# Startup loads in another order, and VectorE makes part of the gate logits of a graph-and-experts layer

## The chip, the cores and the metric

The kernel runs on one core of one Trainium2 chip. Its time is the device time of one execution in microseconds (us); smaller is better. TensorE (PE) does the matmuls, its weight loads are listed as PEld, VectorE is DVE, ScalarE is ACT, GpSimd is POOL. SyncE (SP) computes nothing here: it issues most of the DMAs, one after the other in its queue; ACT and POOL issue the rest.

## The reference

There are 3125 tokens (rows) of 256 numbers and a sparse graph of 53125 weighted edges among them. The layer is

```
xn = layernorm(x)
# graph part, adj[dst, src] += weight
h  = adj @ xn
a0 = softmax((adj @ h) @ W0.T + b0)            # 128 wide
a1 = softmax((adj @ [a0, a0]) @ W1.T + b1)
x  = x + tanh([a0, a1] + h) + linear_attention(xn)
# experts part
xn2 = layernorm(x)
logits = xn2 @ gate_w + gate_b                 # 8 experts, top 1, capacity 489
buf[e, slot] = xn2 of the tokens of expert e
y   = relu(buf @ w1[e] + b1[e]) @ w2[e] + b2[e]   # 256 -> 1024 -> 256
x   = x + y[token] * prob[token]
```

## The kernel before

Everything is in f32 and written out by hand: each engine has one queue of instructions whose order is fixed in the code, and semaphores carry the waits. Tokens are cut into 25 tiles of 128.

**Start.** SP loads all of `dst`; from it DVE works out where in the sorted edge list each tile begins (`base_i`). With these numbers SP loads a window of edges per tile, three small DMAs each (`window`, L436), in four groups of tiles, `GROUPS = ((0, 2), (2, 6), (6, 16), (16, 25))`. Group 0 is written out, the others are loops on SP. Behind group 0 SP issues the loads of `x` (L454, L457) and of five weights (`wo`, `wq`, `W0`, `W1`, `b1`; L461); behind group 1 eleven gate weights, biases and other constants (L451); then groups 2 and 3. All sixteen weights and constants count on one semaphore, `s_w`. ACT loads the first 7 tiles of `x` and two weights at the very start, and then loads its activation table (L670). ACT turns the integers of a group of windows into floats in `cast` (L700 to L702), at the end of the turn before the one in which DVE's `prepare` uses them.

**Build.** A software pipeline over `it`: per turn DVE makes one-hot tiles, PE multiplies them to dense 128x128 blocks of the adjacency matrix (`build`, L1464), ACT copies them out (`evac`) and they are stored to DRAM and at once applied to xn (`apply`, L1481). During the first 25 turns edges are sorted into slots as well (`spread`, `slot`, `ranks`, `slots`), and keys and values are made (`turn`, `product`, `squares`, `kvprod`). PE turns the five weights in `others()`, at `it == 1`, after a wait for all of `s_w`.

**Two layers.** The dense matrix streams back through a ring of five 1280 KB slots (L542), and PE multiplies it per strip of four tiles (`strip(l, k, inserts)`, L1631: 25 steps `j` per strip, two records each). Between the steps of strip `k` of layer 1 PE executes inserts for earlier strips: `turns` (L1647), `gate_turn(k - 1)` at step 23 (8 transposes of finished rows X1, L1385), `logits(k - 2)` at step 2 (16 records, L1667), `counts(k - 2)` at step 10 (L1676 to L1684). ACT copies the transposed rows out (`xtout`, L817). DVE's order for each strip is `chosen(k - 2)` (bias and choice of expert, starts with L1263), `biased(k - 1)` (L1217), `summed`, `finished` (L1233), `moments`, `root`, `slotted(k - 2)`, `prob(k - 2)`, `normal(k - 1)` (L1286, writes the normed rows XN). The last three strips have two, two and one tile and an order of their own. POOL scatters each normed row to its slot of an expert's buffer in DRAM (L636) and its residual row (L643).

**Experts.** After some matmuls whose results are not used (`WARM`, L1733), for each of the 8 experts PE does `up` (L1719, 8 blocks `f` of 128 hidden units), ACT the relu of each block (L864), PE `down` (L1730, four token blocks `c`, 8 steps `f` each), DVE the output rows (`yblock`), POOL the scatter to `out`. SP loads an expert's tokens with `tokens` in four quarters (L515) and their residual rows with `kept_rows` (L518); DVE transposes the tokens in `columns` (L1370).

Of the kernel before, what the change touches and what calls it, by code (L numbers as in the profile page):

```python
# [17 lines left out]
H = 128  # L18
P = 128
NT = 25  # L20
NE = 8
# [26 lines left out]
NWL = 16  # L48
# [14 lines left out]
NGT = len(GATES)  # L63
WARM = 11
# [44 lines left out]
def graph_program(nc, a, out):  # L109
    ctx = ExitStack()  # L110
    with ctx:
# [110 lines left out]

        iota_n = sb("iota_n", [P, P])
# [116 lines left out]
        s_w = sem("s_w")  # L340
        s_wt = sem("s_wt")
# [31 lines left out]
        s_xn2 = sem("s_xn2")  # L373
        s_nb = sem("s_nb")
# [51 lines left out]
        def _(sp):  # L426
# [10 lines left out]
            for g, (t0, t1) in enumerate(GROUPS):  # L437
                if g == 0:
                    for j in range(t0, t1):
                        window(g, j)  # L440
                else:
                    with sp.Fori(t0, t1) as j:
                        window(g, j)
                if g == 1:
                    for to, src in ((gate_w[:, :, :], half("L0_ffn_gate_w")), (bo_b[:, :], a["L0_mix_bo"].partition_broadcast(P)), (gb1_b[:, :], a["L0_gnn_b1"].partition_broadcast(P)),
# [12 lines left out]
                if g == 0:  # L458
                    for to, src in ((wo_n, half("L0_mix_wo")), (wq_n, half("L0_mix_wq")), (W0_n, a["L0_gnn_W0"]),
                                    (W1_n, a["L0_gnn_W1"]), (b1_n, a["L0_ffn_b1"])):  # L460
                        sp.dma_start(to, src).then_inc(s_w, 16)  # L461
# [50 lines left out]
            def tokens(e, s):  # L512
                blocks = xbuf_dram[ds(e * XS, XS), :].rearrange("(b j) (q f) -> q j b f", j=32, q=4)
                for q in range(4):
                    sp.dma_start(xbs[32 * q:32 * q + 32, s, :, :], blocks[q]).then_inc(s_tok[s], 16)  # L515
# [10 lines left out]
            for l in (0, 1):  # L526
                for q in range(NC):
# [14 lines left out]
                    sp.dma_start(RING[:, slot_of[g % 5], 0:w], adj_dram[q, :, 0:w]).then_inc(s_ald[g % 5], 16)  # L542
                    if g == 10:
# [7 lines left out]
            tokens(0, 0)  # L551
            tokens(1, 1)
            sp.wait_ge(s_dres, 16 * NT)
            kept_rows(0, 0)
            before(0, NT)
# [108 lines left out]
        def _(act):  # L664
            half = lambda name: a[name].rearrange("(r p) n -> p r n", p=P)
            act.dma_start(X1[:, 0:XG[0][1], :], a["x"][0:XG[0][1] * P, :].rearrange("(j p) d -> p j d", p=P)).then_inc(s_x[0], 16)
            act.dma_start(wk_n, half("L0_mix_wk")).then_inc(s_kvw, 16)
            act.dma_start(wv_n, half("L0_mix_wv")).then_inc(s_kvw, 16)
            act.wait_ge(s_const, 2)
            nc.scalar.activation(rsum[:, 0, 0:1], ones_f[:, 0:1], ACT.Sqrt)  # L670
# [88 lines left out]
            for it in range(NU + 3):  # L759
# [24 lines left out]
                if it == 1:  # L784
# [25 lines left out]
            def xtout(k):  # L810
# [3 lines left out]
                n, i0 = len(Z1[k]), Z1[k][0] - GATES[g][0]  # L814
                for b in range(i0 // 2, (i0 + n + 1) // 2):
# [944 lines left out]
```

## Time and profile before

| | |
|---|---|
| time, median of 3 runs | 1199.76 us (1198.54 to 1200.06) |
| the profiled execution's own time | 1197.42 us |
| its span in the profile | 1195.6 us |
| PE busy | 1112.7 us, 93% of the span |
| DVE busy | 708.8 us, 59% |
| ACT busy | 316.0 us, 26% |
| POOL busy | 166.6 us, 14% |
| DMA | 175.37 MB, 147 GB/s over the span |

The profile is of one execution. Busy times are sums over the whole span, which has stages with different limits; "idle before" is time that an engine stood still ahead of an instruction, and the arrow behind it names what released it. Ends of matmuls are modelled. The stages are: start and sorting to about 200 us, build to 629, layer 0 to 775, layer 1 to 947, experts to the end.

### The profile page before, as it was taken

Reading aid. Unit: us, or ns where it says so; the run is one execution under the profiler, and the core shown is the slowest. Engines: PE = TensorE matmul, PEld = TensorE weight load, DVE = VectorE, ACT = ScalarE, POOL = GpSimd, SP = SyncE. Lnnn points to the kernel's source line nnn. Section 1 sums busy time; section 2 is a strip of 40 time slices with the busy share of each in tenths; the row PEclk is TensorE's granted clock in tenths of the full one; section 3 lists DMA queues with packets and bytes.
Section 4 is the critical chain, followed back from the end, with each engine's and each line's share of the span. In section 5 each row is a group of like instructions: output and inputs, shape, how many; then the busy total and the mean of one; then the engine's idle time right before and its main releaser. Section 6 shows DMA issues by size and latency. Waiting matters only on the chain.

```text
span 1195.6 us, 14060 instructions
## 1 busy us (share of the span) xinstructions
PE 1112.7 (93%) x4867; PEld 700.0 (59%) x4867; DVE 708.8 (59%) x1563; ACT 316.0 (26%) x1035; POOL 166.6 (14%) x206
## 2 busy tenths in 40 slices
PE   3589989999999999999998999999999699999995
PEld 2356656666666666666683444545558456666664
DVE  7798999998786877768740010204536334554443
ACT  3468767521212212112220111101112111222220
POOL 1013223301010100000000000000333511111111
PEclk9789989999999999999998999999999799999998
DMA  5111110122323333332238988787884564555510
GB/s 162 18 12 46 45 45 18 72 88 90 140 103 139 122 121 127 120 156 94 88 116 318 350 314 306 267 309 267 300 305 149 159 199 113 117 141 131 136 58 7
DMA packets 78724, 175.37 MB, mean 147 GB/s; under 512 B 33567, under 2 KB 62010, under 8 KB 66622
## 3 DMA queue, kind: packets, MB, share of 16 engines
q1 hardware_dynamic: 68462, 124.02, 32.8%
q10 hardware_dynamic: 6064, 42.40, 8.8%
q0 software_dynamic: 4128, 8.04, 1.9%
q8 instruction: 41, 0.67, 0.2%
q14 instruction: 29, 0.24, 0.1%
HBM read 113.82 MB, written 63.09 MB: 148 GB/s over the span
## 4 chain that ended last, share of the span: by engine, by line
PE 80%; DVE 9%; issue 3%; ACT 3%; another core or an unknown queue 2%; SPq 2%; DMA 1%; POOL 0%; POOLq 0%; DVEq 0%; ACTq 0%
PE ps L1481 20%; PE ps L1631 18%; PE ps L1464 11%; PE ps L1730 9%; PE ps L1719 9%; PE ps L1448 2%; PE ps L1507 2%; PE ps L1385 2%; PE ps L1434 2%; DVE W L983 1%; PE ps L1483 1%; PE ps L1733 1%; DVE RY L979 1%; ACT W L715 1%
## 5 line engine op out<-in xcount | busy, mean ns | idle before, releaser
L1481 PE MATMUL ps<-RING,XX 128*128 128x512 f32 x600 | 283.1, 594 | 0.3 <-ACT RING L743 0.3
L1631 PE MATMUL ps<-RING,RY 128*128 128x512 f32 (+2 forms) x750 | 277.5, 527 | 4.6 <-issue 4.6
L1631 PEld LDWEIGHTS ps<-RING,RY 128*128 128x128 f32 x750 | 134.0, 192 | 131.2 <-issue 129.1
L1464 PEld LDWEIGHTS ps<-RING 128*128 128x128 f32 x1250 | 163.7, 193 | 45.8 <-issue 44.7
L743 ACT COPY RING<-ps 128x512 f32<-128x512 f32 (+1 forms) x157 | 91.6, 584 | 317.0 <-PE ps L1464 300.7
L1464 PE MATMUL ps<-RING 128*128 128x128 f32 x1250 | 171.1, 278 | 0.5 <-ACT RING L733 0.5
L1481 PEld LDWEIGHTS ps<-RING,XX 128*128 128x128 f32 x600 | 102.9, 191 | 73.2 <-issue 72.0
L1023 DVE TENSOR_TENSOR RING<-iota_n,RY 128x512 f32<-128x512 f32 (+1 forms) x157 | 108.0, 688 | 43.6 <-PE ps L1464 38.9
L1029 DVE TENSOR_TENSOR RING<-iota_n,RY 128x512 f32<-128x512 f32 (+1 forms) x157 | 117.3, 747 | 0.0
L864 ACT ACTIVATE RY<-ps,b1T 128x489 f32<-128x489 f32 x64 | 42.8, 669 | 179.7 <-PE ps L1719 178.7
L1032 DVE TENSOR_TENSOR RING<-RING,RY 128x512 f32<-128x512 f32 x132 | 90.2, 683 | 0.0
L1358 DVE SCALAR_TENSOR_TENSOR W<-ps,RING,W 128x256 f32<-128x256 f32 (+1 forms) x32 | 15.5, 484 | 111.1 <-PE ps L1730 110.1
L636 POOL DMA_INDIRECT xbuf_dram<-XX,sidx x25 | 24.7, 989 | 345.1 <-DVE sidx L1298 339.6
L1202 DVE TENSOR_REDUCE nmx<-ps 128x4 f32<-128x512 f32 (+1 forms) x7 | 4.4, 634 | 113.9 <-PE ps L1385 113.9
L622 POOL TENSOR_TENSOR XX<-XX,bo_b 128x256 f32<-128x256 f32 x25 | 29.3, 1173 | 255.0 <-PE ps L1464 255.0
L1730 PE MATMUL ps<-RING,RY 128*128 128x256 f32 (+1 forms) x256 | 56.3, 381 | 3.0 <-ACT RY L864 3.0
L1730 PE MATMUL ps<-XT,RY 128*128 128x256 f32 (+1 forms) x256 | 56.3, 381 | 3.0 <-ACT RY L864 3.0
L659 POOL DMA_INDIRECT out<-W,RING x32 | 31.3, 978 | 198.0 <-DVE W L1365 181.3
L1730 PEld LDWEIGHTS ps<-RING,RY 128*128 128x128 f32 (+1 forms) x256 | 47.1, 185 | 13.8 <-ACT RY L864 6.2
L1730 PEld LDWEIGHTS ps<-XT,RY 128*128 128x128 f32 (+1 forms) x256 | 47.1, 185 | 13.7 <-ACT RY L864 6.2
L1719 PE MATMUL ps<-RING,XT 128*128 128x489 f32 x128 | 53.2, 574 | 1.5 <-issue 1.5
L1448 PE MATMUL ps<-wkvT,XT 128*128 128x512 f32 x100 | 50.9, 633 | 4.0 <-ACT XT L706 4.0
(251 smaller groups left out, 1268.3 us busy)
## 6 DMA issues: line engine op xcount, KB each, us to landing
RING<-adj_dram SPq DMA_DIRECT2D x62, 1280.0 KB
adj_dram<-RING ACTq DMA_DIRECT2D x31, 1280.0 KB, 4.6
rbuf_dram<-W SPq DMA_DIRECT2D x8, 516.0 KB, 5.5
RING<-rbuf_dram SPq DMA_DIRECT2D x8, 516.0 KB, 4.1
xbuf_dram<-W SPq DMA_DIRECT2D x8, 512.0 KB, 3.2
XT<-in_L_ffn_w SPq DMA_DIRECT2D x16, 256.0 KB
XT<-in_L_ffn_w SPq DMA_DIRECT2D x4, 1024.0 KB
RING<-in_L_ffn_w SPq DMA_DIRECT2D x16, 256.0 KB
```

Of the source, the lines that this page charges most:

```text
L659: gp.indirect_dma_start(out[:, :], bass.IndirectOffsetOnAxis(ap=rbs[0:n, e % 2, c, D + 1:RES].bitcast(I32), axis=0), ybs[0:n, e % 2, c, :] ...
L743: nc.scalar.copy(RING[:, n % 2, u % 5 * 512:u % 5 * 512 + w], ps[:, u % 2, 0:w]).then_inc(s_bev, 1)
L864: nc.scalar.activation(hmT[:, f, 0:CAPX], ps[:, 2 + f % 3, 0:CAPX], ACT.Relu, bias=b1T[:, f, e:e + 1]).then_inc(s_hidv, 1)
L1023: v.tensor_tensor(h[:, 0, 0:n, :], every, grid(0), ALU.is_equal).then_inc(s_eq, 1)
L1029: last = v.tensor_tensor(h[:, 1, 0:n, :], every, grid(1), ALU.is_equal)
L1032: last = v.tensor_tensor(h[:, 0, 0:n, :], h[:, 0, 0:n, :], grid(2), ALU.mult)
L1448: last = nc.tensor.matmul(ps[:, PROD, :], XT[:, c, m * P:(m + 1) * P], wkvT[:, c, :], start=(c == 0), stop=(c == 1))
L1464: last = nc.tensor.matmul(o[:, i * P:(i + 1) * P], h[:, 0, i, :], h[:, 1, i, :], start=True, stop=(j != s))
L1481: last = nc.tensor.matmul(ps[:, ACC + dd, :], w, at, start=(j == 0), stop=True, skip_group_check=True)
L1631: last = nc.tensor.matmul(o, (Y if l == 0 else S0)[:, j, :], RING[:, slot_of[g % 5], i * across + first:i * across + first + w], start=(j ...
L1719: last = nc.tensor.matmul(ps[:, 2 + f % 3, 0:CAPX], w1s[s][:, c, f * P:(f + 1) * P], xbT[:, s, c, 0:CAPX], start=(c == 0), stop=(c == 1))
L1730: last = nc.tensor.matmul(o, hmT[:, f, c * P:c * P + n], w2s[s][:, f, :], start=(f == 0), stop=(f == 7))
```

## The change

Six edits are made together.

1. ACT loads its activation table ahead of its three DMAs, not behind them.
2. The four windows of group 1 are written out on SP instead of looped over. The five weights go behind them, ahead of the constants, on a semaphore of their own (`s_wt5`); PE waits for these alone, at `it == 2` instead of 1, and ACT's copies move with it.
3. For the first two tiles of each of the first four strips of layer 1, the gate logits come from DVE: a new `dots(k)` after `normal(k)`, 16 multiply-and-add-up instructions over 256 elements. PE's transposes and logits of these tiles, and one of ACT's two copies per strip, are gone. The gate weights come in spread over all partitions (1024 KB, issued on SP in layer 1 behind load `NC + 5` of the ring), and DVE reorders them once.
4. `counts` moves from step 10 (12 in strip `ka`) to step 15.
5. The tokens of expert 0 are issued half on SP and half on ACT, and the residual rows of expert 0 go ahead of the tokens of expert 1.
6. `down` waits for the relu blocks one at a time in its first token block, instead of for all eight ahead of it.

```diff
-NWL = 16
+NWL = 11
+DOTS, DOT_TILES = 4, 2
+        gwb = HB[:, 0:16, 0:H].rearrange("p t (f e) -> p t f e", e=NE)
+        gwT = RY[:, 3250:5298].rearrange("p (e f) -> p e f", e=NE)
+        junk = xtf[:, 6144:6400]
...
@@ SP, start
-                if g == 0:
+                if g < 2:
                     for j in range(t0, t1):
                         window(g, j)
...
                 if g == 1:
+                    for to, src in ((wo_n, half("L0_mix_wo")), (wq_n, half("L0_mix_wq")), (W0_n, a["L0_gnn_W0"]),
+                                    (W1_n, a["L0_gnn_W1"]), (b1_n, a["L0_ffn_b1"])):
+                        sp.dma_start(to, src).then_inc(s_wt5, 16)
...
-                if g == 0:
-                    for to, src in ((wo_n, half("L0_mix_wo")), (wq_n, half("L0_mix_wq")), (W0_n, a["L0_gnn_W0"]),
-                                    (W1_n, a["L0_gnn_W1"]), (b1_n, a["L0_ffn_b1"])):
-                        sp.dma_start(to, src).then_inc(s_w, 16)
@@ SP, ring loads
+                    if g == NC + 5:
+                        sp.wait_ge(s_sum[0], 4)
+                        sp.dma_start(HB[:, 0:16, 0:H], a["L0_ffn_gate_w"].rearrange("f e -> (f e)").partition_broadcast(P).rearrange("p (t r) -> p t r", t=16)).then_inc(s_gwb, 16)
@@ SP, experts
-            tokens(0, 0)
-            tokens(1, 1)
+            tokens(0, 0, (0, 1))
             sp.wait_ge(s_dres, 16 * NT)
             kept_rows(0, 0)
+            tokens(1, 1)
@@ ACT
+            act.wait_ge(s_const, 2)
+            nc.scalar.activation(rsum[:, 0, 0:1], ones_f[:, 0:1], ACT.Sqrt)
             act.dma_start(X1[:, 0:XG[0][1], :], ...).then_inc(s_x[0], 16)
             act.dma_start(wk_n, half("L0_mix_wk")).then_inc(s_kvw, 16)
             act.dma_start(wv_n, half("L0_mix_wv")).then_inc(s_kvw, 16)
-            act.wait_ge(s_const, 2)
-            nc.scalar.activation(rsum[:, 0, 0:1], ones_f[:, 0:1], ACT.Sqrt)
...
-                if it == 1:
+                if it == 2:
                     others_out()
...
+                if k < DOTS:
+                    n, i0 = n - DOT_TILES, DOT_TILES
...
+            act.wait_ge(s_disp, 16 * NT)
+            for q in (2, 3):
+                act.dma_start(xbs[32 * q:32 * q + 32, 0, :, :], ...[q]).then_inc(s_tok[0], 16)
@@ DVE, layer 1
+                if k < DOTS:
+                    dotted = slice(GATES[k][0], GATES[k][DOT_TILES])
+                    v.tensor_tensor(tb8[:, dotted, :], tb8[:, dotted, :], gate_b[:, :].unsqueeze(1).to_broadcast([P, DOT_TILES, NE]), ALU.add)
+                for i, j in list(enumerate(GATES[k]))[DOT_TILES if k < DOTS else 0:]:
...
+            def dots(k):
+                dve.wait_ge(s_xn2, k + 1)
+                for j in GATES[k][:DOT_TILES]:
+                    for e in range(NE):
+                        link(v.scalar_tensor_tensor(out=junk, in0=XN[:, j, :], scalar=1.0, in1=gwT[:, e, :], op0=ALU.mult, op1=ALU.mult, accum_out=tb8[:, j, e:e + 1]))
+            dve.wait_ge(s_gwb, 16)
+            link(v.tensor_copy(gwT.rearrange("p e (t r) -> p t r e", t=16), gwb))
...
                 normal(k - 1)
+                if k - 1 < DOTS:
+                    dots(k - 1)
@@ PE
             def others():
-                pe.wait_ge(s_w, 16 * NWL)
+                pe.wait_ge(s_wt5, 16 * 5)
...
-                if it == 1:
+                if it == 2:
                     others()
...   gate_turn and logits
-                for j in Z1[k]:
+                for j in Z1[k][DOT_TILES if k < DOTS else 0:]:
...
-                    inserts[10] = [later(counts, k - 2)]
+                    inserts[15] = [later(counts, k - 2)]
...   strip ka: counts from step 12 to 15
             def down(e, s):
-                pe.wait_ge(s_hidv, 8 * e + 8)
                 for c in range(4):
...
                     for f in range(8):
+                        if c == 0:
+                            pe.wait_ge(s_hidv, 8 * e + f + 1)
```

## Rows read from the trace of the kernel before

**Rows 1.** The page, busy time of each engine: us, share of span, instructions.
```profile
PE 1112.7 (93%) x4867; PEld 700.0 (59%) x4867; DVE 708.8 (59%) x1563; ACT 316.0 (26%) x1035; POOL 166.6 (14%) x206
```

**Rows 2.** The chain that ended last: start us, us, what.
```profile
36.15 3.07 DMA cols<-in_L_mix_ln_k_b
...
818.40 0.87 PE ps L1385 x8
...
822.71 1.69 PE ps L1667 x16
```

**Rows 3.** Timeline of the start: start us, us, engine line op, idle before and releaser.
```profile
2.41 1.28 ACT L670 ACT_TABLE_LOAD   x1 [2.41 <-issue]
...
6.16 0.18 DVE L907 CAST W<-W 125x17 f32<-125x17 int32 x1 [1.93 <-DMA W<-in_dst]
...
9.41 0.41 SPq L436 DMA_DIRECT2D HB<-in_src  x1
...
11.52 0.34 SPq L436 DMA_DIRECT2D HB<-in_src  x1
...
15.92 2.33 SPq L461 DMA_DIRECT2D RING<-in_L_mix_wo  x1
...
21.63 0.36 SPq L436 DMA_DIRECT2D HB<-in_src  x1
...
24.23 0.35 SPq L436 DMA_DIRECT2D HB<-in_src  x1
...
32.82 0.20 DVE L946 TENSOR_SCALAR W<-HB 128x72 f32<-128x72 f32 x1 [4.51 <-ACT HB L702]
...
37.70 0.37 SPq L436 DMA_DIRECT2D HB<-in_src  x1
...
51.69 0.27 DVE L893 RECIPROCAL lna<-lnr 128x18 f32<-128x18 f32 x1 [3.39 <-ACT lnr L689]
...
65.38 0.34 SPq L436 DMA_DIRECT2D HB<-in_edge_weight  x1
...
67.27 0.33 ACT L700 CAST HB<-HB 128x180 f32<-128x180 int32 x1
...
69.15 0.40 DVE L995 RECIPROCAL hta<-hrs 128x40 f32<-128x40 f32 x1
```

**Rows 4.** Busy time of each engine in one stretch of layer 1, clock, DMA.
```profile
778.00:803.00 25.00, 25.00 (x66) 11.58 (x65) 0.00 (x0) 0.58 (x1) 0.00 (x0) 1.00 0.86 312
```

**Rows 5.** Instructions of two DVE lines: count, ns least/median/most, span of starts.
```profile
L1128 DVE SCALAR_TENSOR_TENSOR HB<-HB x1: 628/628/628, 328.9 to 328.9; 128x450 bf16<-128x450 f16 x1
L1128 DVE DVE_READ_ACCUMULATOR HB<-HB x1: 84/84/84, 329.4 to 329.4; 128x1 f32 x1
...
L1362 DVE SCALAR_TENSOR_TENSOR W<-W x32: 424/426/427, 978.7 to 1185.0; 128x256 f32<-128x256 f32 x24, 105x256 f32<-105x256 f32 x8
```

**Rows 6.** Timeline of layer 1, as rows 3.
```profile
824.43 0.63 DVE L1263 SCALAR_TENSOR_TENSOR wkvT<-ps,wkvT,gate_b 128x8 f32<-128x8 f32 x4 [9.83 <-PE ps L1667]
...
876.39 0.63 DVE L1263 SCALAR_TENSOR_TENSOR wkvT<-ps,wkvT,gate_b 128x8 f32<-128x8 f32 x4 [10.54 <-remote]
...
899.90 0.63 DVE L1263 SCALAR_TENSOR_TENSOR wkvT<-ps,wkvT,gate_b 128x8 f32<-128x8 f32 x4 [8.35 <-remote]
...
908.41 1.09 PE L1385 MATMUL ps<-ident,XX 128*128 128x128 f32 x8 [0.41 <-DVE XX L1233]
...
938.73 0.79 PE L1647 MATMUL ps<-W1T,W 128*128 128x128 f32 x2 [5.32 <-ACT W L795]
```

**Rows 7.** Timeline from layer 1 to the experts.
```profile
953.55 4.32 SPq L515 DMA_DIRECT2D RING<-xbuf_dram  x8
...
958.84 1.30 DVE L1370 STREAM_TRANSPOSE RING<-RING 128x512 f32<-128x512 f32 x2 [10.28 <-DMA RING<-xbuf_dram]
...
959.70 13.36 PE L1719 MATMUL ps<-RING,XT 128*128 128x489 f32 x32 [1.54 <-issue]
```

**Rows 8.** Groups by line: busy, mean ns, idle before, releaser.
```profile
L1730 PE MATMUL ps<-XT,RY 128*128 128x256 f32 (+1 forms) x256 | 56.3, 381 | 3.0 <-ACT RY L864 3.0
```

More of the change, by code:

```diff
@@ L340, in graph_program @@
         s_w = sem("s_w")
+        s_wt5 = sem("s_wt5")
         s_wt = sem("s_wt")
@@ L373, in graph_program @@
         s_xn2 = sem("s_xn2")
+        s_gwb = sem("s_gwb")
         s_nb = sem("s_nb")
@@ L510, in weights, with tokens @@
                 sp.dma_start(w2s[s], a["L0_ffn_w2"][ds(e, 1), :, :].rearrange("a (c p) f -> p (a c) f", p=P)).then_inc(s_wl[s], 16)
-            def tokens(e, s):
+            def tokens(e, s, quarters=(0, 1, 2, 3)):
                 blocks = xbuf_dram[ds(e * XS, XS), :].rearrange("(b j) (q f) -> q j b f", j=32, q=4)
-                for q in range(4):
+                for q in quarters:
                     sp.dma_start(xbs[32 * q:32 * q + 32, s, :, :], blocks[q]).then_inc(s_tok[s], 16)
@@ L864, in hidden @@
                     nc.scalar.activation(hmT[:, f, 0:CAPX], ps[:, 2 + f % 3, 0:CAPX], ACT.Relu, bias=b1T[:, f, e:e + 1]).then_inc(s_hidv, 1)
+            act.wait_ge(s_disp, 16 * NT)
+            for q in (2, 3):
+                act.dma_start(xbs[32 * q:32 * q + 32, 0, :, :], xbuf_dram[0:XS, :].rearrange("(b j) (q f) -> q j b f", j=32, q=4)[q]).then_inc(s_tok[0], 16)
             for e in range(NE):
@@ L1261, in chosen @@
                 dve.wait_ge(s_lg, k + 1 if k < NGT - 1 else NZ)
-                for i, j in enumerate(GATES[k]):
+                if k < DOTS:
+                    dotted = slice(GATES[k][0], GATES[k][DOT_TILES])
+                    v.tensor_tensor(tb8[:, dotted, :], tb8[:, dotted, :], gate_b[:, :].unsqueeze(1).to_broadcast([P, DOT_TILES, NE]), ALU.add)
+                for i, j in list(enumerate(GATES[k]))[DOT_TILES if k < DOTS else 0:]:
                     last = v.scalar_tensor_tensor(out=tb8[:, j, :], in0=ps[:, LGB, i * NE:(i + 1) * NE], scalar=nr[:, 1, j:j + 1], in1=gate_b[:, :],
@@ L1663, in logits @@
                 ge(pe, s_lgr, g)
-                for j in Z1[k]:
+                for j in Z1[k][DOT_TILES if k < DOTS else 0:]:
                     i = j - GATES[g][0]
@@ L1701, in _ @@
                 strip(1, k, inserts)
-            strip(1, ka, {1: [later(logits, ka - 2)], 3: [later(turns, 1, ka - 1)], 12: [later(counts, ka - 2)], 21: [later(gate_turn, ka - 1)]})
+            strip(1, ka, {1: [later(logits, ka - 2)], 3: [later(turns, 1, ka - 1)], 15: [later(counts, ka - 2)], 21: [later(gate_turn, ka - 1)]})
             strip(1, kb, {3: [later(turns, 1, ka)], 4: [later(logits, ka - 1)], 14: [later(counts, ka - 1)], 22: [later(gate_turn, ka)]})
```

## The prediction

> **What bounds the kernel now.** I read the page first, then the chain that ended last, then the timeline at the places that the edits touch. The page says that PE is busy for 93% of the span [rows 1], so in the build and in the two layers only less work on PE, or an end to one of its waits, pays. The chain says where PE isn't the bound. At the start it goes through SP's queue and ends in the landing of the last constant at 39.2 us, for which PE's `others()` waits [rows 2]. Late in layer 1 it turns into DVE's work on the gate, and in the experts it is PE again, with a short ACT step between `up` and `down`. So four places matter: the start, the gate's share of PE in layer 1, the step to the experts, and that ACT step. I take each by itself, as PE's or DVE's order joins them in one line: what comes earlier at one place stays earlier behind it.
>
> **The start.** PE's 12 us wait for the constants looks like the prize, but it isn't all to be had. Follow what is late next. With the wait gone, the first turns go as fast as DVE and the windows allow, and DVE waited in two places: 4.51 us for the cast of group 1, whose windows now come earlier, and 3.39 us for ACT's root, which was late behind PE at 32.82 and 51.69 [rows 3], 7.9 us together. But ACT's `cast` of group 2 starts at 67.27, when the last DMA of that group, issued at 65.38, has just landed (1.9 us) [rows 3]. Before the change that load had nothing to spare, so from here on the start can only gain what SP's queue gains. DVE's step behind the cast (69.15) shows no idle time ahead of it: DVE and the windows were level.
>
> What SP's queue gains up to the first window of group 2, at 37.70 [rows 3]:
> - The four windows of group 1. In the loop one starts 2.60 us after the other (21.63 to 24.23), written out 2.11 us (9.41 to 11.52) [rows 3]. 4 x 0.49 = 2.0 us.
> - `dst`. DVE waits 1.93 us for it, until 6.16 [rows 3], and all of SP's queue hangs on this. It shares the DMA engines with the three loads that ACT issues at once; now these come behind the 1.28 us table load [rows 3]. Bounds 0 and 1.93 (DVE isn't free sooner); I take 1.5, since `dst` is by far the smallest of them and needs only a little lead.
> - The weight `wo` takes 2.33 us to issue, a window's DMA 0.34 to 0.41 [rows 3]: SP is held up behind the large loads of x. Behind the windows it may cost little; or the first window pays in its place. Bounds 0 and 2.0, I take 0.8, between the two.
> - The order of the five weights and the constants costs nothing more: all were ahead of 37.70 already.
>
> Sum 4.3 us, bounds 2.0 and 5.9; I add 0.2, as DVE then waits for the windows where it was level with them: 4.5 us. The cover of the rest: ACT's x, `wk` and `wv` come some 1 to 2 us later and push DVE's first work back by as much, which the 7.9 us less the 4.5 us hold. `others()` at turn 2 is 15 short PE records while DVE still prepares group 1; its weights are issued right behind the windows of group 1 and land about when that work starts. Group 3's windows come as much earlier on the same queue. The build after it is bound by PE and DVE and keeps the 4.5 us.
>
> **The gate in layer 1, what PE sheds.** Eight transposes take 0.87 us, sixteen logit records 1.69 us [rows 2], 2.56 us per strip; half of it goes in four strips: 4 x 1.28 = 5.1 us. One of ACT's two copies goes too, off the path.
>
> **What DVE pays.** `dots` is 16 linked instructions per strip, each a SCALAR_TENSOR_TENSOR over 256 f32 with an accumulator read. The same instruction without the read takes 426 ns; the one pair in the trace takes 628 ns for 450 elements and its 84 ns read ends with it [rows 5]. Both fit one line of (628 - 426) / 194 = 1.05 ns per element, so the read seems hidden. With the 0.03 us that a linked neighbour starts later: 0.46 us. If the read came in full behind it, 0.54. I take 0.48, nearer to the pair: 16 x 0.48 = 7.7 us per strip. They stand behind `normal`, where DVE idles before `chosen` for 9.8, 10.5 and 8.4 us [rows 6] (three of the four stand there). PE now delivers the logits 1.28 us earlier, so 8.5, 9.2 and 7.1 us are free. The first three groups fit. The fourth doesn't: `chosen(3)`, at 899.90, can move up by 3 x 1.28 = 3.84 us from the strips before, and in its own strip by 8.35 - 7.7 = 0.65 us instead of 1.28. That matters, because from there the path is DVE's: PE waits 0.41 us for DVE's `finished` at 908.41 [rows 6]. So layer 1 gains 3.84 + 0.65 = 4.5 us; 4.9 at 0.46 us per dot, 3.5 at 0.54.
>
> `counts` at step 15 lies later than one-hot rows that come earlier than now, so PE doesn't wait in it, and `slotted`, which needs it, stands behind `root`: nothing. The 1 MB of gate weights (1024 KB) and DVE's reordering (2048 elements, 3.4 us at eight times the 426 ns row) fall where DVE is idle for 25 us and the DMA engines are 0.86 busy at 312 GB/s [rows 4]. At that rate the extra MB takes 3.4 us in a ring whose loads are asked for four chunks of ten records ahead, 15 us at 66 records in 25 us [rows 4]. Hidden; without the ring's lead it would be 3.4 us once. SP waits for `s_sum` there, which layer 0 has long given.
>
> The Trainium skill speaks against this edit: its page "Vector Engine (DVE) Microarchitecture Reference", section "Points that are easy to get wrong", says that this instruction with two SBUF sources that aren't bf16 halves its throughput. L1362 is such an instruction, without an accumulator, and a slope of 1.05 ns from a bf16 pair to it shows no halving; with the accumulator on f32 no run here shows it. By the rule the sum is the second rival's.
>
> **To the experts.** PE waits 1.54 us after its unused matmuls, until DVE's transpose has begun on expert 0's tokens; DVE waits for the last of four quarters, issued 0.54 us apart (8 in 4.32 us) [rows 7]. With two on each queue the last is issued 1.1 us earlier, and expert 1's no longer follow on its heels. Bounds 0 (the landing is what takes the time, not the issue) and 1.54; I take 1.0. Expert 1's tokens now wait for the residual scatter, which is done well before PE has finished expert 0.
>
> **`down`.** PE stands still 3.0 us for the relu in this group and 3.0 in its twin over the other weight buffer [rows 8], 6.0 in all, 0.76 per expert. The relu of block 7 is the last; seven of the eight steps of the first token block now stand in front of it, and it has only 0.76 us left to run. All 6.0 us go. Seven more waits per expert on PE's queue cost at most what the like waits in `up` do, where no idle time is listed. DVE's output rows wait for PE, not the other way round: what hides them stays.
>
> **The sum.** 4.5 + 4.5 + 1.0 + 6.0 = 16.0 us. The profiled execution took 1197.42 us around its span of 1195.6, 2.3 below the median of the runs; the saving is a difference, so I put it on the median: 1199.76 - 16.0 = 1183.8 us.
>
> **Rivals.**
> 1. *SP's queue stays as long.* `dst` lands no earlier and the wait of `wo` only moves to the windows: the start gives 2.0, and with dots at 0.54 us layer 1 gives 3.5: 12.5 us, 1187.3. For it: every byte of x still has to pass. Chance 0.18.
> 2. *The accumulating form runs at half rate.* The streaming part, 256 x 1.05 = 0.27 us, doubles: 0.46 + 0.27 = 0.73 us per dot, 11.7 per strip. Then DVE never idles between groups: from `chosen(2)` at 876.39 to the end of its work at 891.55 is 15.2 us, so a group takes 26.9, and from 814.60 (824.43 - 9.83) `chosen(3)` starts at 814.6 + 11.7 + 3 x 26.9 = 907.0, 7.1 later than before. 4.5 + 1.0 + 6.0 - 7.1 = 4.4 gained: 1195.4. Against it: rows 5. Chance 0.08.
> 3. *The other side: dots that take more than 0.81 us each.* In that formula `chosen(3)` is late by 64 c - 39.8 us; it eats the other 11.5 us from c = 0.80. At twice the whole row, 0.85 + 0.03 = 0.88, it is 16.5 late: 5 us slower, 1204.8. Chance 0.04.
> 4. *A stall that goes.* Near 933 us PE, DVE, ACT and SP all stand still; PE for 5.32 us before 938.73 [rows 6], and ACT, named as releaser, was waiting too. Nothing in the profile explains it. If the new order of PE's work clears it, 4.6 us more: 1179.2. Chance 0.08.
> 5. *The start isn't bound where I think*, and the edits give back what they gain to within a measurement. Chance 0.02.
>
> The forecast has 0.60: its own range is 1181 to 1187. To reach 8 in 10 I take in rivals 1 and 4: 1178.5 to 1191. A measurement of this kernel can tell about 0.2%, 2.4 us. Faster by more: 0.60 + 0.18 + 0.08 + 0.08 = 0.94; within: 0.02; slower: 0.04.
>
> **What would show it.** Right: group 2's cast near 62.8 with ACT idle ahead of it; dots at 0.46 to 0.50 us apart; `chosen(3)` directly behind the last of them, and the first three with idle time before them; PE waiting about 1.3 us for `finished(4)`; no idle time at L1730; a gap under 0.8 us before the first `up`. Wrong: a cast near 65 (rival 1), dots apart by over 0.6 us, PE idle in the ring while the gate weights load, or a clock below full speed in the early turns, if PE now stands still longer before the group 2 windows.

## The result, and the profile after

The changed kernel takes 1177.26 us, median of four runs (1176.02 to 1178.36), beside 1199.15 us for the kernel before on the same chip: a ratio of 0.9818, 95% interval 0.9801 to 0.9835, or 21.9 us less. The prediction was 16.0 us less, 1183.8, with 1178.5 as its low end: the direction was right, the size too small. The profiled execution took 1178.36 us around a span of 1176.6, so the two traces stand 19.0 us of span apart (the traced execution of the kernel before, 1197.42 us, is faster than all of its four runs, that of the changed kernel is the slowest of its four).

The page of the changed kernel, busy time of each engine:

```profile
PE 1109.7 (94%) x4819; PEld 697.4 (59%) x4819; DVE 738.8 (63%) x1688; ACT 315.3 (27%) x1031; POOL 167.6 (14%) x206
```

DVE has 30 us more work than in [rows 1], nearly all of it the new dots (64 of 0.467 us). The start, in the timeline of the changed kernel, answers to [rows 3]:

```profile
0.81 1.28 ACT L676 ACT_TABLE_LOAD   x1 [0.81 <-PEq L1778]
1.25 0.44 ACTq L677 DMA_DIRECT2D XX<-in_x  x1
...
5.04 0.30 DVE L921 CAST W<-W 125x17 f32<-125x17 int32 x1 [0.80 <-DMA W<-in_dst]
...
8.43 0.41 SPq L443 DMA_DIRECT2D HB<-in_src  x1
...
15.67 1.39 SPq L443 DMA_DIRECT2D HB<-in_src  x1
...
20.78 0.35 SPq L443 DMA_DIRECT2D HB<-in_src  x1
...
22.81 0.35 SPq L443 DMA_DIRECT2D HB<-in_src  x1
...
24.16 0.43 SPq L454 DMA_DIRECT2D RING<-in_L_mix_wo  x1
...
34.35 0.37 SPq L443 DMA_DIRECT2D HB<-in_src  x1
...
59.41 0.34 SPq L443 DMA_DIRECT2D HB<-in_edge_weight  x1
...
61.07 0.34 ACT L709 CAST HB<-HB 128x180 f32<-128x180 int32 x1 [3.12 <-DMA HB<-in_edge_weight]
...
62.56 0.40 DVE L1009 RECIPROCAL hta<-hrs 128x40 f32<-128x40 f32 x1 [2.33 <-ACT hrs L781]
```

`dst` lands 1.1 us earlier (DVE had waited for it until 6.16, now until 5.04), although ACT's load of x is issued during the table load and not behind it. The windows of group 1, written out, stand 2.03 us apart. The issue of `wo` fell from 2.33 to 0.43 us, but the first window of group 1 now pays 1.39. Group 2's first window comes 3.35 us earlier, its last DMA 5.97 (65.38 to 59.41), and the cast 6.2 (at 61.07, where the prediction had 62.8), with 3.12 us of idle time on ACT ahead of it.

DVE in layer 1: the last dot of the first group, then `chosen(0)`; the last dot of the fourth group, then `chosen(3)`; and PE at `gate_turn(4)`:

```profile
813.51 0.42 DVE L1327 SCALAR_TENSOR_TENSOR XT<-XX,RY 128x256 f32<-128x256 f32 x1
813.86 0.08 DVE L1327 DVE_READ_ACCUMULATOR XT<-XX,RY 128x1 f32 x1
815.04 0.17 DVE L1278 TENSOR_TENSOR wkvT<-wkvT,gate_b 128x16 f32<-128x16 f32 x1 [1.09 <-PE ps L1694]
...
885.90 0.42 DVE L1327 SCALAR_TENSOR_TENSOR XT<-XX,RY 128x256 f32<-128x256 f32 x1
886.36 0.17 DVE L1278 TENSOR_TENSOR wkvT<-wkvT,gate_b 128x16 f32<-128x16 f32 x1
...
895.43 1.09 PE L1412 MATMUL ps<-ident,XX 128*128 128x128 f32 x8 [0.88 <-DVE XX L1247]
```

The picture is the forecast one: idle time behind the first group's dots, none behind the fourth's, PE 0.88 us late for `finished(4)`. Against [rows 6] `chosen(3)` comes 13.5 us earlier, 8.1 of it the start's (the transpose for which PE waits at the start of layer 1 is at 775.11 and 766.98). That leaves 5.4 us for layer 1 up to there, where the sum had 4.5. But 1.7 of the 5.4 are a delay that is gone, not work saved. In the kernel before, on this chip, DVE began `chosen(3)` (899.90) 1.69 us after PE's logits were done:

```profile
896.36 1.85 PE L1667 MATMUL ps<-gate_w,XT 128*128 128x8 f32 x16
```

The reorder of the gate weights took DVE 2.35 us, at 782.10, and PE has no idle time in the ring there.

Then something that the change isn't about. The timeline of PE and ACT, and below it the stretch behind the stall (us, busy time of PE, PEld, DVE, ACT, POOL, granted clock, DMA share, GB/s):

```profile
910.83 0.60 PE L1412 MATMUL ps<-ident,XX 128*128 128x128 f32 x4
...
915.61 0.59 ACT L828 COPY XT<-ps 128x512 f32<-128x512 f32 x1 [9.72 <-remote]
...
917.46 0.90 PE L1674 MATMUL ps<-W1T,W 128*128 128x128 f32 x4 [4.05 <-issue]
```

```profile
917.00:925.00 8.00, 7.54 (x38) 7.54 (x39) 1.25 (x4) 1.25 (x5) 4.41 (x5) 0.57 0.18 61
```

The unexplained stall of [rows 6] is still there, one strip earlier and 4.05 instead of 5.32 us long, and behind it the clock is granted at 0.57, that is mostly at the lower level of 1.2 GHz, for 8 us of work. PE, ACT and DVE stand still; POOL goes on issuing its scatters. ACT begins to copy PE's transposes out 4.2 us after they are done (911.43 to 915.61), and the profile names only "remote" as what released it. At the end of layer 1 the lead over the kernel before is 10.2 us (`counts` at 946.76 and 936.60), at `gate_turn(4)` it was 13.0.

The step to the experts in PE's timeline, and `down` in the groups by line, as in [rows 7, 8]:

```profile
948.93 13.36 PE L1746 MATMUL ps<-RING,XT 128*128 128x489 f32 x32
```

```profile
L1758 PE MATMUL ps<-XT,RY 128*128 128x256 f32 (+1 forms) x256 | 55.9, 379 | 0.0
```

No idle time ahead of it, nor in its twin. The first `up` is 10.8 us earlier than at 959.70 [rows 7], the end 19.0: the eight experts alone gave 8.2 us.

### The profile page after: what moved, and what is told of

The parts are those of the page before. It is cut to its first block, busy times and chain, and to the rows that moved or that the text cites. A ratio compares the mean times of both kernels' runs of the same rounds, so it can differ in the third digit from the quotient of the medians.

```text
span 1176.6 us, 14070 instructions
## 1 busy us (share of the span) xinstructions
PE 1109.7 (94%) x4819; PEld 697.4 (59%) x4819; DVE 738.8 (63%) x1688; ACT 315.3 (27%) x1031; POOL 167.6 (14%) x206
## 4 chain that ended last, share of the span: by engine, by line
PE 81%; DVE 8%; SPq 4%; issue 3%; ACT 2%; another core or an unknown queue 1%; DMA 0%; POOL 0%; POOLq 0%; DVEq 0%; ACTq 0%
PE ps L1508 20%; PE ps L1658 19%; PE ps L1491 11%; PE ps L1758 9%; PE ps L1746 9%; SPq L443 2%; PE ps L1534 2%; PE ps L1475 2%; PE ps L1461 1%; PE ps L1412 1%; PE ps L1761 1%; PE ps L1510 1%; DVE W L997 1%; SPq L441 1%
## 5 line engine op out<-in xcount | busy, mean ns | idle before, releaser
L1658 PEld LDWEIGHTS ps<-RING,RY 128*128 128x128 f32 x750 | 136.4, 196 | 131.0 <-issue 128.8
L1746 PE MATMUL ps<-RING 128*128 128x489 f32 x128 | 53.1, 573 | 0.0
```

The lines of the kernel that those rows point to most:

```text
L1658: last = nc.tensor.matmul(o, (Y if l == 0 else S0)[:, j, :], RING[:, slot_of[g % 5], i * across + first:i * across + first + w], start=(j ...
L1746: last = nc.tensor.matmul(ps[:, 2 + f % 3, 0:CAPX], w1s[s][:, c, f * P:(f + 1) * P], xbT[:, s, c, 0:CAPX], start=(c == 0), stop=(c == 1))
```

## The experiments

They ran in five goes, each beside runs of the kernel before on its own chip: chip B (before: 1189.61 us), C (1189.21), D (1197.6), C again (1189.06) and E (1200.48). The first comparison's chip is called A; it may be one of D and E. Ratios are to before on the same chip.

**One part at a time, chip B.** a1_down has this edit alone:

```
 def down(e, s):
-    pe.wait_ge(s_hidv, 8 * e + 8)
...
+        if c == 0:
+            pe.wait_ge(s_hidv, 8 * e + f + 1)
```

> The kernel before with one edit: in each expert `down` waits for the relu block by block instead of for all eight. By the prediction's step only the idle time ahead of `down` goes, 0.76 us for each of 8 experts: 6.0 us, and an expert takes 27.2 us instead of 28.0. By the theory formed on the two traces, the first weight load of `down` was also behind the wait and could not lie beside a matmul, so that the wait cost about 1.03 us each: 8.2 us, and an expert takes 26.9. Nothing ahead of 940 us may differ from before; PE's unexplained pause then still ends near 938.

a2_start:

```
-if g == 0:
+if g < 2:
     for j in range(t0, t1):
         window(g, j)
...
 if g == 1:
+    for to, src in ((wo_n, half("L0_mix_wo")), (wq_n, half("L0_mix_wq")), (W0_n, a["L0_gnn_W0"]),
+                    (W1_n, a["L0_gnn_W1"]), (b1_n, a["L0_ffn_b1"])):
+        sp.dma_start(to, src).then_inc(s_wt5, 16)
...
+nc.scalar.activation(rsum[:, 0, 0:1], ones_f[:, 0:1], ACT.Sqrt)
 act.dma_start(X1[:, 0:XG[0][1], :], a["x"][0:XG[0][1] * P, :].rearrange("(j p) d -> p j d", p=P)).then_inc(s_x[0], 16)
...
-if it == 1:
+if it == 2:
     others()
```

The five weights are no longer behind group 0, and PE waits for `s_wt5` alone.

> The kernel before with the edits of the start alone: the table load ahead of the loads of x, the five weights behind the windows of group 1 on a semaphore of their own, group 1 written out, and others() at turn 2. By the prediction's sum 4.5 us are gained and the cast of group 2 starts near 62.8 us. By the trace of the changed kernel it is about 7.8 us by the end of the build, the cast starts near 61.1, and the loop of group 2 takes 2.54 us per window instead of 2.79. If part of the gain came from edits elsewhere, the build ends less than 7 us earlier. Whether the pause of PE near 933 us moves with it (to 925) or jumps to some other place tells if it hangs on the time since the start or on where the engines stand in the program.

a3_gate: it has `DOTS, DOT_TILES = 4, 2` with `dots(k)`, the gate weights' load and copy, and `counts` at step 15.

> The kernel before with the edits of the gate alone: DVE makes the logits of two tiles in each of four groups, and counts at step 15. If the order of the work in layer 1 alone moves the pause of PE, it shows near 921 us with 4 us and slow matmuls behind it, and the gain is 4.85 - 3.0 = 1.9 us. If the pause stays as it was before, the gain is about 4.85 us (the prediction's step said 4.5).

a4_tokens:

```
-tokens(0, 0)
-tokens(1, 1)
+tokens(0, 0, (0, 1))    # quarters 2 and 3 on ACT's queue
...
 kept_rows(0, 0)
+tokens(1, 1)
```

> The kernel before with the edit of the tokens alone: two quarters of expert 0's tokens on ScalarE's queue, expert 1's behind the kept rows. By the prediction the idle time of PE ahead of the first up falls from 1.54 us to about 0.5, a gain of 1.0 us. By the rival that the landing takes the time and not the issue, nothing. By the trace of the changed kernel 1.2 us or more may be had, at most the 1.54. In the times it is within the measurement; the profile decides.

| | median us | ratio, 95% | less than before | predicted |
|---|---|---|---|---|
| a1_down | 1181.5 | 0.9932, 0.9915 to 0.9948 | 8.1 | 6.0 |
| a2_start | 1183.06 | 0.9942, 0.9925 to 0.9958 | 6.6 | 4.5 |
| a3_gate | 1185.75 | 0.9964, 0.9949 to 0.9978 | 3.9 | 4.5 |
| a4_tokens | 1188.34 | 0.9988, 0.9979 to 0.9998 | 1.3 | 1.0 |

The parts add up to 19.8 us before rounding. In the traces, a1_down has no idle time ahead of `down`, and an expert takes 26.93 us where it takes 27.96 in c_before, 1.03 less; a2_start's cast starts at 61.02 and its loop step is 2.53 us; a4_tokens leaves 0.56 us ahead of the first `up`. And in none of the four is there a stall near 933 us, nor anywhere else in layer 1.

**The whole on another chip, and the loop on SP, chip C.** c_before and c_after are the two kernels unchanged. c_loop is a2_start with `if g == 0` left as it was. c_shift is the kernel before with

```
+if g == 2:
+    for _ in range(12):
+        sp.wait_ge(s_zero, 1)    # long satisfied
 with sp.Fori(t0, t1) as j:
```

> The kernel before once more, for its trace beside the others of this chip. If PE's pause near 933 us belongs to the program, it is there with some 5 us on whichever chip this is, and the time is near 1199. If it belongs to a chip or its surroundings, it may be missing, and the time is then near 1190, as in the runs of the kernel before beside the last four experiments.

> The changed kernel once more. The parts alone gave 8.1 (down), 6.6 (start), 3.9 (gate) and 1.3 us (tokens), 19.9 in all. If they add up and the pause of PE is missing on this chip, the ratio is 0.983 to 0.984. If the start gives more together with the others than alone, as the 21.8 us of the first comparison would have it, 0.982. By the prediction's terms, 16.0 us, it would be 0.9866.

> The edits of the start without the one that writes group 1 out: the table load and the order of the weights only, with group 1 in its loop as before. The prediction put 2.0 us on this one edit, so 6.6 - 2.0 = 4.6 us should be left. SP then has as many instructions ahead of the loop of group 2 as in the kernel before. If the step of that loop, 2.79 us before and 2.54 after, hangs on where the loop stands in SP's program, it is 2.79 again, and 2.5 us more are lost: 2.1 us left. If it hangs on what else is under way at that time, it stays at 2.54.

> The kernel before with twelve waits that are long satisfied on SP, between the constants and the loop of group 2, and nothing else. They cost SP some tenths of a us. If the step of the loop hangs on where it stands in SP's program, it can now be 2.54 us instead of 2.79, and the cast of group 2 starts up to 2 us earlier than in the kernel before in spite of the added waits. If the step has to do with the data or with other engines' work, it stays at 2.79 and the cast comes later by what the waits cost.

c_before took 1188.76 us, with no stall. c_after: 1168.93 us, ratio 0.9827 (0.9811 to 0.9844), 20.3 us less. The two traces of this chip give the cleanest pair. The timeline of c_before at the cast of group 2, the transpose for which PE waits at the start of layer 1, the last `counts` and the first `up`:

```profile
67.01 0.33 ACT L700 CAST HB<-HB 128x180 f32<-128x180 int32 x1
...
773.73 0.33 PE L1385 MATMUL ps<-ident,W 128*128 128x128 f32 x1 [1.17 <-ACT W L793]
...
938.11 0.20 PE L1676 MATMUL ps<-wkvT,upto_b 128*128 128x24 bf16 x1 [3.30 <-DVE wkvT L1277]
...
951.04 4.34 PE L1719 MATMUL ps<-RING,XT 128*128 128x489 f32 x10 [1.28 <-DVE RING L1370]
```

and the same four of c_after:

```profile
61.02 0.34 ACT L709 CAST HB<-HB 128x180 f32<-128x180 int32 x1 [3.35 <-DMA HB<-in_edge_weight]
...
767.68 0.33 PE L1412 MATMUL ps<-ident,W 128*128 128x128 f32 x1 [1.18 <-ACT W L802]
...
927.83 0.20 PE L1703 MATMUL ps<-wkvT,upto_b 128*128 128x24 bf16 x1 [2.57 <-DVE wkvT L1294]
...
940.06 13.36 PE L1746 MATMUL ps<-RING,XT 128*128 128x489 f32 x32 [0.22 <-DVE RING L1397]
```

Differences: 5.99, 6.05, 10.28 and 10.98 us, and 19.2 at the ends of the spans (1186.9 and 1167.7). So start 6.05, gate 4.23, tokens 0.70, experts 8.22.

c_loop: 1184.68 us, ratio 0.9966 (0.9952 to 0.998), 4.5 less. Group 2's loop, and its cast:

```profile
41.65 0.36 SPq L437 DMA_DIRECT2D HB<-in_src  x1
...
44.45 0.36 SPq L437 DMA_DIRECT2D HB<-in_src  x1
```

```profile
65.13 0.34 ACT L700 CAST HB<-HB 128x180 f32<-128x180 int32 x1 [7.88 <-DMA HB<-in_edge_weight]
```

The step is 2.8 us again, as expected if the loop's speed comes with the writing out of group 1, and the cast is 4.1 us later than in c_after. But the expectation's 2.1 us gained were 4.5, and only 1.8 us of the cast's lateness are left at the start of layer 1 (769.48). The last pair, below, takes this up. c_shift: 1189.69 us, ratio 1.0004 (0.9994 to 1.0014), step 2.77: the loop's place in SP's program was not what counted, or 12 was the wrong number.

**Place or not, the fourth group of dots, and a candidate, chip D.** d_shift24 has 24 such waits, d_after_shift is the changed kernel with 12; d_dots3 has `DOTS, DOT_TILES = 3, 2`; d_unroll2 has `if g < 3` in place of `if g < 2`.

> The kernel before with 24 satisfied waits on SP ahead of the loop of group 2 instead of 12. With 12 the step of the loop was 2.77 us, so that they did not settle what the step hangs on. If it hangs on where the loop stands in SP's program, some number of added instructions brings 2.54 us, and 24 may be one; if it stays at 2.77 to 2.79 again, the place alone is unlikely.

> The changed kernel with 12 satisfied waits on SP ahead of the loop of group 2. Its loop takes 2.54 us per window. If the place in SP's program decides, it may become 2.79 here; if what decides is that group 1 is written out and no loop runs ahead of it, it stays at 2.54. The waits themselves cost SP some 0.4 us; by the end of the start that may show as 0.4 us, or as up to 2.9 with the slower step.

> The changed kernel with dots in three groups instead of four. The prediction gave the fourth 0.65 us, since in its strip DVE has idle time for nearly all of the 7.7 us. From the last two traces of one chip, chosen(3) came 9.8 us earlier, of which the start had given 6.0 and the three strips before give 3.84: nothing is left for the fourth. Then chosen(3) starts at the same time as in the changed kernel within 0.1 us, now with some 7 us of idle time ahead of it instead of directly behind the last dot, and the time stays the same. By the prediction's term it is 0.65 us later.

> The changed kernel with group 2's ten windows written out as well. Written out, a window follows the other after 2.03 us, in the loop after 2.54, so the last is issued 5.1 us earlier. In the changed kernel the first work behind the cast of group 2 waits 2.97 us on DVE and 3.35 on ACT. If those idle times are all that the cast's lateness costs, 3.0 us are gained (ratio to before 0.980 where the changed kernel has 0.983); the rival is that the windows of group 3 or DVE's build then hold the rest back and less than 1 us comes through.

Windows of group 2 in d_shift24, then in d_after_shift:

```profile
41.59 0.35 SPq L436 DMA_DIRECT2D HB<-in_src  x1
...
44.34 0.35 SPq L436 DMA_DIRECT2D HB<-in_src  x1
```

```profile
40.55 0.35 SPq L443 DMA_DIRECT2D HB<-in_src  x1
...
43.09 0.35 SPq L443 DMA_DIRECT2D HB<-in_src  x1
```

2.75 us in the first, 2.54 in the second. By a count of SP's program that no trace shows, the loop stands behind 75 instructions in d_shift24 and 77 in d_after_shift, behind 63 in c_shift (2.77 us) and 65 in the changed kernel (2.54). So the place alone is unlikely to decide it. Their single times are 1200.18 and 1176.57 us.

d_dots3: 1176.85 us. In its trace PE's last logits for `chosen(3)` and DVE:

```profile
883.95 1.85 PE L1694 MATMUL ps<-gate_w,XT 128*128 128x8 f32 x16
```

```profile
887.51 0.63 DVE L1280 SCALAR_TENSOR_TENSOR wkvT<-ps,wkvT,gate_b 128x8 f32<-128x8 f32 x4 [7.78 <-remote]
```

PE was done at 885.8, but DVE moved 1.7 us later. By PE's end, `chosen(3)` could have come 71.05 us after `chosen(0)` (814.75); with four groups, in d_after_shift, it comes 71.33 after (815.62 to 886.95). So where DVE starts at once the fourth group gives nothing, not 0.65 us. As DVE was late here, `chosen(3)` came 72.76 us after, and the fourth group was worth 1.4 at that place. It doesn't show in the single times, 1176.85 and 1176.57 us.

This lateness belongs to the chip too. In all five traces of A, D and E that leave DVE without dots ahead of `chosen(3)` (the kernel before, d_shift24, d_dots3, f_start, f_loop), DVE starts 1.7 to 2.7 us after PE's logits are done. In the six of B and C (c_before, a1_down, a2_start, a4_tokens, c_loop, c_shift) it starts within 0.04.

d_unroll2: 1174.85 us, ratio 0.9802 (0.9784 to 0.982).

On this chip the stall is back, in all four traces: 4.29 us before 929.69, 5.48 before 926.72, 5.48 before 926.98 and 5.87 before 924.37.

**The candidates beside the changed kernel, chip C.** e_after is the changed kernel, e_unroll2 the same as d_unroll2, e_unroll3 has `if g < 4` (all windows written out), e_loop0 has `if g == 1` (group 0 looped, group 1 written out).

> The changed kernel, to be set against the three next ones on the same chip. On the chips without PE's pause near 933 us its ratio was 0.983, on the first one, which has the pause, 0.982.

> The changed kernel with group 2's windows written out too. Its last run gave 1174.85 us beside 1176.6 and 1176.9 for two single runs of kernels close to the changed one, and its cast of group 2 came at 57.34 instead of 61.04, with the build's end 3.1 us earlier. If that comes through, it is 2 to 3 us faster than the changed kernel beside it; if the late pauses of PE and DVE take it back, less than 1.

> The changed kernel with all windows written out, group 3 too. Group 3's windows are issued 2.56 us apart in the loop and 2.03 written out, but its cast comes much later; if the load of group 3 has slack, as the lack of idle time around its cast says, this gives nothing over the kernel with group 2 written out. If it is late by some us, up to 2 us more.

> The changed kernel with group 0's two windows in a loop and group 1's written out, so that a loop again runs ahead of group 2's. With 77 instructions ahead of it, the loop of group 2 took 2.54 us per window in the changed kernel and with 75 it took 2.75 in the kernel before, so that its place alone does not decide. If a loop that ran ahead makes the step long, it is near 2.79 here; if it takes a loop directly ahead, or something else of group 1's loop, it stays at 2.54.

| | median us | ratio, 95% |
|---|---|---|
| e_after | 1168.8 (1168.53 to 1170.13) | 0.983, 0.9816 to 0.9843 |
| e_unroll2 | 1166.8 (1165.62 to 1167.82) | 0.9815, 0.9802 to 0.9829 |
| e_unroll3 | 1165.99 (1165.84 to 1166.74) | 0.9808, 0.9794 to 0.9821 |
| e_loop0 | 1168.37, one run | |

Written out, group 2's cast comes at 57.71 in e_unroll2 instead of 60.78 in e_after, without idle time on ACT ahead of it. 2.0 us of that come through, and no run of e_unroll2 is as slow as the fastest of e_after. Writing out group 3 as well gives 0.8 more by the medians, which five runs don't part. The step in e_loop0 is 2.54, so that a loop ran ahead is not by itself enough to make it slow.

**The start with and without group 1 written out, chip E.** f_start is a2_start again, f_loop is c_loop again.

> The edits of the start alone once more, now beside the version that leaves group 1 in its loop, on one chip. It gave 6.6 us on another chip (5.0 to 8.9 by its interval), and 6 us in the traces: 5 to 8 here.

> The same without the edit that writes group 1 out. It gave 4.5 us (2.4 to 5.7) though its cast of group 2 came only 1.9 us earlier than in the kernel before and 4.1 us later than with all edits. If the later cast costs the time that it is late, f_loop is 4 us behind f_start, and the slower step of group 2's loop is what the prediction's sum missed. If only some 2 us of it reach the end, as predicted for this edit, the missed part of the start is in the table load and the order of the weights, and the loop's step is a side issue.

f_start: 1192.39 us, ratio 0.9931 (0.9911 to 0.995), 8.1 less. f_loop: 1195.01 us, ratio 0.9955 (0.9937 to 0.9973), 5.5 less. The casts are 4.4 us apart (61.10 and 65.50), the median times 2.6 (the two sets of runs overlap), the starts of layer 1 1.5 (766.48 and 767.97). Two stretches behind the cast show where the rest went, for f_start (columns as above):

```profile
66.00:75.00 9.00, 4.63 (x16) 1.85 (x16) 8.73 (x20) 4.79 (x24) 0.01 (x1) 0.94 0.12 13
75.00:84.00 9.00, 9.00 (x43) 6.96 (x43) 8.90 (x13) 3.32 (x9) 1.62 (x3) 0.68 0.11 11
```

and for f_loop:

```profile
66.00:75.00 9.00, 5.12 (x11) 3.03 (x12) 7.60 (x25) 6.36 (x30) 0.53 (x2) 0.50 0.12 11
75.00:84.00 9.00, 7.45 (x46) 4.58 (x45) 8.90 (x11) 5.38 (x26) 2.19 (x3) 0.95 0.13 14
```

Both have a stretch at the lower level of the clock, 1.2 GHz, behind an idle time of PE. In f_loop PE had stood still for 7.58 us ahead of 69.88, and the slow stretch lies where PE waits for the cast's followers anyway (0.50 from 66 to 75). In f_start it lies on the next turn's matmuls (0.68 from 75 to 84), which PE does without a pause. From one L1422 (a matmul that each turn has once) to the next that turn takes 11.6 us (72.29 to 83.94) in f_start, 8.7 in f_loop: 2.9 us of f_loop's delay are given back there. That isn't fixed by the kernel, though. c_loop is the same kernel as f_loop, PE waits 7.82 us at the same place, and there the turn takes 10.6 us, with a second slow stretch in it (0.57 from 81 to 84 us).

## Why the prediction was too small

**`down`: the term that the traces of C have furthest off, 8.2 instead of 6.0.** The step that failed reads "PE stands still 3.0 us for the relu in this group and 3.0 in its twin ... 6.0 in all ... All 6.0 us go." The mechanism was right, but the listed idle time is not what the wait costs. PE's weight loads around the wait in c_before, and the matmuls:

```profile
991.38 0.19 PEld L1719 LDWEIGHTS ps<-RING 128*128 128x128 f32 x1 [0.22 <-issue]
993.12 0.19 PEld L1730 LDWEIGHTS ps<-RING,RY 128*128 128x128 f32 x1 [1.55 <-ACT RY L864]
```

```profile
984.82 7.54 PE L1719 MATMUL ps<-RING 128*128 128x489 f32 x18
993.12 1.13 PE L1730 MATMUL ps<-RING,RY 128*128 128x256 f32 x4 [0.76 <-ACT RY L864]
```

and in a1_down:

```profile
991.12 0.19 PEld L1719 LDWEIGHTS ps<-RING 128*128 128x128 f32 x1 [0.22 <-issue]
991.53 0.19 PEld L1731 LDWEIGHTS ps<-RING,RY 128*128 128x128 f32 x1 [0.22 <-issue]
```

```profile
991.94 2.32 PE L1731 MATMUL ps<-RING,RY 128*128 128x256 f32 x10
```

Without the wait, a weight load follows each 0.41 us and its matmul 0.41 behind it. So without the wait `down` would have started at 991.38 + 0.41 + 0.41 = 992.20 in c_before; it started at 993.12, 0.92 late. The listed 0.76 counts from the modelled end of the last matmul of `up`, and that end (573 ns after its start) lies 0.16 behind the start of the next one in an unbroken row. The first matmul of `down` starts together with its weight load and takes up to 484 ns, not 379: another 0.11. 0.92 + 0.11 = 1.03 us per expert, 8.2 in all, which a1_down's time (8.1) and each pair of traces bear out.

**The start: 6.6 and 8.1 us by a2_start's and f_start's times instead of 4.5.** The failed step is "from here on the start can only gain what SP's queue gains", in two ways. First, the queue was followed only to group 2's first window. Up to the first constant the sum came out; these are its issue in the kernel before and in the changed one:

```profile
30.93 0.40 SPq L451 DMA_DIRECT2D gate_w<-in_L_ffn_gate_w  x1
```

```profile
26.54 0.39 SPq L461 DMA_DIRECT2D gate_w<-in_L_ffn_gate_w  x1
```

That is 4.4 us, where the sum said 4.3. But "the order of the five weights and the constants costs nothing more" was wrong: from there to group 2's first window SP took 7.81 us, not 6.77, so that 3.35 us were left (on C 8.34 and 6.76 us, and 1.97 left). In return the loop took 2.54 us per step and not 2.79, nine steps, 2.3 us, and nothing in the sum stood for that; so the cast came 6.0 to 6.2 us earlier. Apart from a first or a single longer turn, the step is 2.74 to 2.80 in all the kernels that loop group 1 and 2.53 to 2.54 in all that write it out and loop group 2, on every chip. It isn't a loop ahead as such, and hardly the place; what it is stays open.

Second, the cast's time and the time of the whole are not the same thing. Two turns behind the cast, near 80 and 155 us, hold stretches at the lower clock, and how much of them falls on PE's work differs by kernel and by trace: in c_before these two turns take 10.8 and 11.2 us, in c_after 10.6 and 11.4, in c_loop 10.6 and 10.0, in f_start 11.6 and 10.0, in f_loop 8.7 and 10.1; the turns between take the same in each (6.9, 8.3 once and 10.0 once). The idle time of PE between build and layer 0, 4.1 to 4.7 us, does the same to layer 0's first 66 matmuls. In c_before, then in c_loop:

```profile
632.59 31.32 PE L1631 MATMUL ps<-RING,RY 128*128 128x512 f32 x66 [4.14 <-issue]
```

```profile
629.41 30.26 PE L1631 MATMUL ps<-RING,RY 128*128 128x512 f32 x66 [4.65 <-issue]
```

The clock granted from 634 to 644 us was 0.79 in the first and 1.00 in the second. So the edits that c_loop has give 1.9 us at the cast and 2.4 behind the turn near 80; the turn near 155 adds 1.2, the idle time ahead of layer 0 takes 0.5, and the head of layer 0 adds 1.1, which is the 4.25 us by which layer 1 starts earlier than in c_before (c_loop's time: 4.5). About half of that gain is where the slow stretches fell. Writing group 1 out gives 4.1 to 4.4 us at the cast and 2.6 in the time (chip E), by the same trade: c_after leads c_loop by 4.1 us behind the turn near 80, by 2.7 behind the one near 155 and by 1.8 at the start of layer 1. On A the cast came 6.2 us earlier, layer 1 8.1, and the two slow turns make 1.3 of the difference. One pair of traces can't size the start to better than some 1.5 us.

**The gate: 4.5 predicted, 4.23 in the traces of C, 3.9 by a3_gate's time.** A dot takes 0.467 us (0.42 and a read of 0.08 half hidden) where 0.48 was taken, and 16 take 7.4. By `chosen(3)` the strips before gave 3.7 of their 3.84 (C: 9.8 less the start's 6.05); the 0.65 of the fourth is not there where DVE starts at once.

The rival of half rate falls. The Trainium skill ("Vector Engine (DVE) Microarchitecture Reference", "Points that are easy to get wrong") says that this form halves its throughput with two SBUF sources that aren't bf16; by it the dots were estimated at 0.73 us. This trace doesn't agree with it. The 0.42 us of these f32 instructions with accumulator are the same as the 0.426 of [rows 5] without one. And the prediction's "bf16 pair" was misread: L1128 reads f16 (its slope is 202 / 194 = 1.04 ns per element). Rows with two bf16 sources are elsewhere in the trace of the kernel before:

```profile
L957 DVE SCALAR_TENSOR_TENSOR HB<-HB 128x180 bf16<-128x180 bf16 x1 | 0.3, 340 | 0.0
...
L957 DVE SCALAR_TENSOR_TENSOR HB<-HB 128x36 bf16<-128x36 bf16 x1 | 0.2, 189 | 0.0
```

(340 - 189) / 144 = 1.05 ns per element, which gives 0.42 us for 256: what f32 takes. No run has bf16 sources together with an accumulator.

**To the experts: 1.0 predicted, 0.7 in the traces of C, 1.3 (0.2 to 2.5) by a4_tokens' time.** The idle time of 1.3 to 1.5 us falls to 0.2 (c_after) and 0.56 (a4_tokens).

**The stall (rival 4) doesn't come from the program alone.** It is in all eight traces of chips A, D and E, 4 to 6 us long, at `turns` of one of two neighbouring strips, and in none of the twelve traces of B and C, the same two kernels among them. The kernel before takes 1197.6 to 1200.5 us on the first kind and 1189.1 to 1189.6 on the second. The gain of the whole is there without it: 20.3 us on C, twice. On A it was 21.9 with an interval (19.8 to 23.9) that holds 20.3, and the traced executions are 19.1 us apart, as on C (19.3). So it is not shown that the change is worth more on A. What differs there in the traces is DVE's late `chosen(3)`, 1.7 us that the dots now cover, and the lead of 2.8 us that goes around the stall.

So by the traces of C the change is 6.0 + 4.2 + 0.7 + 8.2 = 19.1 us of span, by its times 20.3, and on A 21.9. The gate and the step to the experts came close to their terms. `down` was priced 2.2 us too low, by a wrong measure of the wait. The start was priced 1.5 to 3.6 us too low: of its terms `dst` and the windows held roughly, the one for the constants was wrong, the loop's faster step was missing, and the slow stretches of the clock moved. The rest of the miss is 0.6 us because the forecast stood on 1199.76 where the comparison has 1199.15, and what A's 21.9 has over C's 20.3, which the runs don't tell from chance. Together they put the time 1.2 us under the low end of the range.

## What to carry to other kernels

To price a wait, don't read the idle time: take the distance between the starts on either side of it and subtract the distance of an unbroken row, and add what the first instruction behind it takes longer. A queue's gain is counted to the last transfer that someone waits for, and behind it the stretches of low clock that the wait leaves, since they move too. SP's windows cost 2.03 us written out, 2.54 or 2.79 in a loop, so a short loop of DMAs on the way to the first work is worth writing out (for group 2, 2.0 us of the whole). And the same kernel should be traced on a second chip before a stall in its profile is taken for its own.

## What the runs showed of the hardware

- Two kinds of chip: on A, D and E PE, ACT and DVE stand still once for 4 to 6 us late in layer 1 while POOL goes on issuing, DVE, where it idles, starts `chosen(3)` 1.7 to 2.7 us after PE's logits are done, and the kernel before is 8 to 11 us slower; on B and C there is none of this. The trace names no cause.
- The same loop on SP took 2.54 us per turn in some programs and 2.74 to 2.79 in others, for all its turns but one or two longer ones; the cause stays open.
- After an idle time of PE the clock was granted at the lower level for a stretch of the work behind it: 0.50 for f_loop's 66 to 75 us. Where PE has to wait anyway, such a stretch is free; where it falls on work it cost 1 to 3 us: the turn near 80 us took 8.7 in f_loop, 10.6 in c_loop (the same kernel on another chip) and 11.6 in f_start.
- DMAs that stand behind ACT's table load in the program are issued during it: the first at 1.25 us, 0.44 after the load's start, though it lasts until 2.09.
- A SCALAR_TENSOR_TENSOR of DVE takes 1.05 ns per element with two bf16 sources, and 0.42 us for 256 elements in f32, with the accumulator or without.
